# Sums for the relations' matrices made beside Wout and root instead of inside the attention, and stored by SyncE

## The reference

```python
# attention (16 heads, 256 random features), xn = layernorm(x)
q, k, v = split(xn @ Wqkv + bqkv)
out = numerator / (denominator + 1e-6)          # per head, feature map exp
x_mix = out @ Wout + bout
# relations
u = xn @ root + bias
for r in range(8):
    mask = (edge_type == r)
    sums = segment_sum(xn[src] * mask[:, None], dst)
    cnt  = segment_sum(mask, dst)
    u = u + (sums / maximum(cnt, 1)[:, None]) @ weight[r]
z = concat([u, xn]) @ w_gate + b_gate
x = x + tanh(u) * z + xn * (1 - z) + x_mix
```

## Time and profile before

| | |
|---|---|
| median of three executions | 3250.0 us |
| lowest, highest | 3239.06, 3251.52 us |
| the profiled execution's time | 3249.8 us |
| its span | 3248.0 us |
| its mean granted TensorE clock | 0.94 of full speed |

### The profile page before, as it was taken

One profiled execution on the slowest core, in us unless ns is written; L12 is line 12 of the kernel. 1 busy time (PEld: TensorE's weight loads), 2 busy tenths in 40 slices (PEclk: granted clock), 3 DMA queues, 4 the chain that ended last, 5 costly groups with the idle time before them and its releaser, 6 DMA issues.

```text
span 3248.0 us, 39307 instructions
## 1 busy us (share of the span) xinstructions
PE 2798.1 (86%) x16055; PEld 2453.6 (76%) x16055; DVE 1869.4 (58%) x2046; ACT 1321.4 (41%) x1721; POOL 582.8 (18%) x535
## 2 busy tenths in 40 slices
PE   4766798899999999999556777779899999999988
PEld 3654587877777777776556766677899999999987
DVE  5438924587877887777725555554244444444443
ACT  1315512266667676667235555541111111112221
POOL 3775400100000000000105555540100000000000
PEclk7889998999999999999768888889999999999999
DMA  4150011699999999989543333443332222113211
GB/s 133 48 139 4 1 48 46 187 320 332 327 323 330 339 325 320 332 313 327 134 169 97 108 102 101 108 116 109 111 90 72 72 72 72 52 52 136 72 60 68
DMA packets 163910, 500.77 MB, mean 154 GB/s; under 512 B 45615, under 2 KB 58287, under 8 KB 162470
## 3 DMA queue, kind: packets, MB, share of 16 engines
q1 hardware_dynamic: 98698, 389.85, 34.6%
q0 software_dynamic: 49312, 74.20, 9.1%
q10 hardware_dynamic: 15722, 34.22, 3.0%
HBM read 425.52 MB, written 72.39 MB: 153 GB/s over the span
## 4 chain that ended last, share of the span: by engine, by line
PE 66%; DVE 9%; ACT 7%; POOL 6%; DMA 5%; issue 4%; another core or an unknown queue 3%; ACTq 0%; SPq 0%; DVEq 0%; POOLq 0%
PE ps L188 65%; POOL scr_edges L926 3%; DMA er<-in_wd 3%; DVE es_l L213 2%; DVE T_l L213 1%; ACT es_h L655 1%; POOL lc L1253 1%; ACT et L2016 1%; DVE acc L209 1%; ACT lh L1213 1%; DMA wr<-in_Wq 1%; POOL scr_adj L1880 1%; DVE x L201 1%; ACT kp_h L2017 1%
## 5 line engine op out<-in xcount | busy, mean ns | idle before, releaser
L213 DVE TENSOR_TENSOR es_l<-er,es_h 128x1408 fp32r<-128x1408 f32 (+1 forms) x455 | 653.1, 1445 | 187.4 <-ACT es_h L655 183.9
L655 ACT ACTIVATE es_h<-er 128x1408 fp32r<-128x1408 f32 (+1 forms) x455 | 563.3, 1242 | 264.7 <-PE ps L188 185.3
L188 PE MATMUL ps<-T_h,ws_h 128*128 128x314 f32 x1856 | 439.5, 319 | 35.1 <-DVE ws_l L213 24.5
L655 ACT ACTIVATE ws_h<-wr 128x1024 fp32r<-128x1024 f32 (+1 forms) x181 | 190.5, 1053 | 631.8 <-PE ps L188 564.0
L188 PE MATMUL ps<-T_h,ws_l 128*128 128x314 f32 x1856 | 432.2, 315 | 0.0
L188 PE MATMUL ps<-T_l,ws_h 128*128 128x314 f32 x1856 | 431.9, 315 | 0.0
L188 PEld LDWEIGHTS ps<-T_h,ws_h 128*128 128x128 f32 x1856 | 325.4, 199 | 40.3 <-issue 28.0
L213 DVE TENSOR_TENSOR ws_l<-wr,ws_h 128x1024 fp32r<-128x1024 f32 x165 | 204.4, 1240 | 233.9 <-ACT ws_h L655 232.0
L188 PEld LDWEIGHTS ps<-T_l,ws_h 128*128 128x128 f32 x1856 | 323.9, 197 | 0.0
L188 PEld LDWEIGHTS ps<-T_h,ws_l 128*128 128x128 f32 x1856 | 322.5, 197 | 0.0
L188 PE MATMUL ps<-es_h,xe_h 128*98 128x512 f32 (+1 forms) x768 | 208.0, 379 | 9.9 <-DVE es_l L213 6.9
(11 more groups left out here) (395 smaller groups left out, 5489.8 us busy)
## 6 DMA issues: line engine op xcount, KB each, us to landing
er<-in_wg SPq DMA_DIRECT2D x128, 704.0 KB, 6.7
er<-in_wu SPq DMA_DIRECT2D x128, 704.0 KB, 5.9
er<-in_wd SPq DMA_DIRECT2D x176, 512.0 KB, 5.1
wr<-in_rel SPq DMA_DIRECT2D x64, 512.0 KB, 3.7
wr<-in_Wqkv SPq DMA_DIRECT2D x24, 512.0 KB, 7.0
steps<-scr_adj POOLq DMA_DIRECT2D x8, 1533.2 KB, 23.8
wr<-in_gate SPq DMA_DIRECT2D x16, 512.0 KB, 3.5
wr<-in_w SPq DMA_DIRECT2D x14, 512.0 KB, 3.5
```

The lines of the kernel that those rows point to most:

```text
L188: return e.matmul(out, l, r, start=start, stop=stop, skip_group_check=True)
L213: return e.tensor_tensor(lo, src, hi.bitcast(F32), ALU.subtract)
L655: q.e.activation(c.hi, c.at, ACT.Copy).then_inc(*self.s("high").up(c.key))
```

## The change

- The tallies leave the attention. They go into slots: one slot after each group of three matmuls (a block and a node tile) of `Wout`, 80 in all, and one after each of the eight steps k of a `root` output, 64 in all. Chunk c takes slot c + 8, so the last one takes slot 130 of 144, in the seventh root output.
- While `Wout` runs, a tally takes two single banks of the three that are left, and VectorE sums each half by itself (`tally_halves`). From slot 80 on it takes an aligned pair, and the sum is one instruction.
- `blocks()` goes through the 16 weight chunks (8 of Wout, 8 of root) with the tallies that fall to each. ScalarE makes the `bod` of the next block ahead. `bod` has six buffers and `blc` eight, `acc` four as before.
- The low parts of seven of these 16 chunks are made by GpSimd (`pool=`, `p_low`).
- SyncE stores the sums: `reg_load` of the row number into a register, then a plain DMA to `d_adj[ds(v, 125), :]`. The stores of a block stand in SyncE's program between the loads of weight chunks. `brows` now holds the first row of each block alone.
- x stays in its place; its copy, the reload and `scr_x` are gone. The tally's buffers lie in R3 instead. The edges' table `seb` is read after the attention's last feature (`p_tallies`).
- ScalarE issues the loads of `nat` directly after the attention (its `a_attention` no longer ends with Wout's splits).
- GpSimd's load of `steps` and the first mean wait until all stores have landed.
- bout is added as a column in the gate (`gated`, one scalar operand more) and no longer as a row on x.

```diff
@@ memory @@
-        X = self.oX
         for i in range(4):
-            at(f"bod{i}", X + i * 1280, NT, BF16)
-            at(f"blc{i}", X + 5120 + i * 256, 128, BF16)
-            at(f"acc{i}", X + 6144 + i * 2528, NT)
+            at(f"acc{i}", R3 + 20224 + i * 2528, NT)
+        for i in range(6):
+            at(f"bod{i}", R3 + 30336 + i * 1280, NT, BF16)
+        for i in range(8):
+            at(f"blc{i}", R3 + 38016 + i * 256, 128, BF16)
@@ weights @@
-                W.add(("Wout", h, i), W2(a["Wout"], 2 * i, 2 * i + 2, h), 1024, 2)
+                W.add(("Wout", h, i), W2(a["Wout"], 2 * i, 2 * i + 2, h), 1024, 2, pool=i % 2 == 0 and h + i > 0)
-            W.add(("root", o), a["root"][o], 1024, 2)
+            W.add(("root", o), a["root"][o], 1024, 2, pool=o % 2 == 0)
@@ sync, for each weight chunk @@
+            n = self.W.of[c.key] - self.W.of["Wout", 0, 0] - 4
+            if 0 <= n < 16:
+                self.s_store_tallies(q, [*blocks[n - 1][2][3:], *blocks[n][2][:3]] if n else blocks[n][2][:3])
+            elif n == 16:
+                self.s_store_tallies(q, blocks[15][2][3:])
@@ new @@
+    def blocks(self):
+        keys = [("Wout", h, i) for h in range(2) for i in range(4)] + [("root", o) for o in range(KD)]
+        n = 0
+        for b, key in enumerate(keys):
+            size = 10 if b < 8 else 8
+            yield b, key, [c for c in range(n - 8, n + size - 8) if 0 <= c < NCH]
+            n += size
+    def s_store_tallies(self, q, chunks):
+        e, m = q.e, self.m
+        for c in chunks:
+            q.wait_ge(self.s("slots"), "rows")
+            e.reg_load(self.slots[c % 4], m["brows"][0:1, c:c + 1])
+            v = e.snap(self.slots[c % 4], min_val=0, max_val=(NBK + NCH) * TP)
+            for i, _, _ in self.tally_halves(c):
+                q.wait_ge(*self.ps.done(("tally", c), i))
+            e.dma_start(self.d_adj[bass.ds(v, TP), :], m[f"acc{c % 4}"][0:TP, :]).then_inc(*self.landed(f"tally{c % 4}").up(c))
@@ t_tally @@
+        if slot < 80:
+            bs = ps.take(("tally", c), 2)
+        else:
+            b, = ps.take(("tally", c), 1, 2)
+            bs = [b, b + 1]
...
+            ins = mm(q.e, ps.one(bs[h], TP, 0, H), m[f"blc{c % 8}"][:, 0:TP], m[f"bod{c % 6}"][:, h * H:(h + 1) * H], True, True)
@@ p_attention becomes p_tallies @@
-        e.dma_start(self.d_x, self.x).then_inc(*self.landed("x_kept").up(0))
...
-                e.indirect_dma_start(self.d_adj, to, m[f"acc{c % 4}"][0:TP, :], None).then_inc(*self.landed(f"tally{c % 4}").up(c))
...
-        e.dma_start(self.x, self.d_x).then_inc(*self.landed("x_back").up(0))
@@ v_relations @@
+        for b, key, chunks in self.blocks():
...
+            for i in range(max(len(chunks), 5)):
+                if b == 4 and i < T:
+                    self.v_add_x1(q, ("Wout", 0), 0, i)
+                if i < len(chunks):
+                    self.v_tally(q, chunks[i])
+                if i == 4:
+                    self.v_low(q, key)
@@ p_relations @@
         q.wait_ge(self.s("product"), ("Wout", 1, 3))
+        for i in range(4):
+            q.wait_ge(self.landed(f"tally{i}"), NCH - 1 - (NCH - 1 - i) % 4)
@@ v_gate @@
-            tt(e, m[f"t3{o % 2}"], t1, t2, ALU.add).then_inc(*self.s("gated").up(o))
+            stt(e, m[f"t3{o % 2}"], t1, m["bcol"][:, 48 + o:49 + o], t2, ALU.add, ALU.add).then_inc(*self.s("gated").up(o))
```

More of the change, by code:

```diff
@@ L704, in t_trn, with t_nat @@
             ins = mm3(q.e, outs, (hi[:, c], lo[:, c]), self.Tk(k, name), k == 0, k == KD - 1)
-        ins.then_inc(*self.s("product").up(key))
-    def t_nat(self, q, name, h, nk, lhs, ready=None, more=()):
+            if k == KD - 1:
+                ins.then_inc(*self.s("product").up(key))
+            if slot is not None:
+                self.t_tally(q, slot + k)
+        self.ps.held = set()
+    def t_nat(self, q, name, h, nk, lhs, ready=None, more=(), slot=None):
         group = (name, *more, h)
+        if slot:
+            was = self.ps.group[(name, *more, 0)]
+            self.ps.held, self.ps.next = set(range(8)) - set(was), was[0]
         bs = self.ps.take(group, T)
+        if slot is not None:
+            self.ps.held = set(bs)
         for i in range((nk + 1) // 2):
@@ L1826, in v_tally @@
+    def v_tally(self, q, c):
         m, ps = self.m, self.ps
[L1827 to L1834, removed]
+        acc, was = m[f"acc{c % 4}"][0:TP, :], m[f"acc{(c - 1) % 4}"][0:TP, :]
+        q.wait_ge(self.s("tallied"), c)
+        if c > 3:
+            q.wait_ge(self.landed(f"tally{c % 4}"), c - 4)
+        for i, cut, src in self.tally_halves(c):
+            shape = two if len(src.shape) == 3 else (lambda z: z)
@@ L1835, in v_tally @@
             if c:
-                q.wait_ge(*ps.done(("tally", c - 1)))
-                ins = stt(q.e, two(acc), two(was), m["same"][0:TP, c:c + 1], src, ALU.mult, ALU.add)
-            else:
-                q.wait_ge(self.landed("x_kept"), 0)
-                ins = q.e.tensor_copy(two(acc), src)
-            ins.then_inc(*ps.out(("tally", c)))
+                for j, _, _ in self.tally_halves(c - 1):
+                    q.wait_ge(*ps.done(("tally", c - 1), j))
+                ins = stt(q.e, shape(acc[:, cut]), shape(was[:, cut]), m["same"][0:TP, c:c + 1], src, ALU.mult, ALU.add)
+            else:
+                q.wait_ge(self.s("attended"), 7)
+                ins = q.e.tensor_copy(acc[:, cut], src)
@@ L1843, in v_slots @@
+            ins.then_inc(*ps.out(("tally", c), i))
     def v_slots(self, q):
@@ L2298, in a_relations @@
             e.dma_start(m[b][0:TP, :].bitcast(F32), self.d[n][0:TP, :]).then_inc(*self.landed("norm_by_nodes").up(i))
[L2299 to L2302 removed]
+        blocks = list(self.blocks())
+        for b, key, _ in blocks:
+            self.a_high(q, key)
+            if not b:
+                self.a_signs(q, blocks[0][2])
+            ahead = blocks[b + 1][2] if b < 15 else []
+            self.a_signs(q, ahead[:6])
+            if b > 7:
+                self.a_root(q, b - 8)
+            self.a_signs(q, ahead[6:])
         for r in range(8):
```

203 lines of the change are left out of this document (87 added, 116 removed).

## The result

The kernel after takes 3316.53 us (median of 3 runs, 3312.0 to 3331.26), the kernel before 3250.0. The ratio is 1.0225 with a 95% interval of 1.0165 to 1.0286: the change makes the kernel slower, clear of noise, by some 2%. The forecast was 3354 with a range of 3262 to 3450. The profiled execution of after is the median one, with a span of 3314.7 us.

A forecast was written before the change was run, and what follows sets the result against it. No engine was full: attention's TensorE waited in order for tally operands; after the move, five DMA engines would pace the stores. 3249.8 - 6 (copy of x) - 140 (attention) + 250.6 (Wout-root stage) = 3354 us, range 3262 to 3450.

The forecast's parts named there:

- The sign and its cause: Whole kernel: slower (chance 0.82), since direct 125-row stores in Wout and root run on five DMA engines, 2.43 us each.
- The attention's term: Attention without its tallies: 17.5 us a round won, 140 us in all, bounds 82 and 263, practical end 190.
- no chain of ScalarE, then VectorE, then TensorE allows: Attention: upper bound of 33 us a round or 263, with every idle microsecond, pairs and clock drops gone, held unreachable.
- eight rounds of 18 tallies: Attention: 18 tallies taken out of each round; 17.5 us a round was counted as 140 us in all.
- The copy of x: Ahead of the attention: dropping the copy shortens ScalarE's wait for the norms' stores by 6 us, bounds 0 and 19.
- The stage: Start of Wout to the count-in: 375.7 us in place of 125.1, +250.6; stores 299, reload 38, weights 17, end 21.7.
- are covered by the same 2.43: Wout and root: stores' waits block loads queued behind them in SyncE, but add nothing beyond 2.43 us a store.
- the engines alone would go at some 1.1 us a tally: Wout with slots: compute engines' pace for `blc`, `bod`, pair and sum, with 0.73 us of Wout between slots.
- my 1.6 for the engines: Wout and root: 1.6 us a tally, as pair, semaphores and first half of a sum come in turn in three banks.
- The register: SyncE's register load before each store: between nothing and 1.25 us, under the 2.43 of the transfer either way.
- The rival that pays: Wout and root: stores spread over 16 engines, 1.6 us a tally, stage 227 us, kernel 3206 us; chance 0.14.
- What was to show it: Signs: attention rounds some 52 us, clock above 0.9, DMA share near 0.33, `acc` 2.4 us apart, `steps` in 16 us.

The follow-up runs named there:

- The last two experiments: Kernel before, tallies kept but nothing stored: 3197.93 us; the same with TensorE's tally matmuls also taken out: 3098.36 us.
- the first experiment: Changed kernel with each sum stored by two DMAs, of 112 and 13 rows, in place of one of 125: 3218.21 us, ratio 0.9911.
- the kernel before with cuts: Kernel before, tallies left in the attention, norms' stores, their reload and `steps` cut into 112 and 13 rows: 3212.77 us, ratio 0.9883.
- the kernel with all cuts: Changed kernel with tally stores, norms' stores, reload and `steps` cut into 112 and 13 rows, row registers loaded by eight: 3147.05 us, ratio 0.9692.

## Why the prediction was right and where it was off

**The sign and its cause were right.** The stores run on five engines: share 0.32 to 0.38, and cutting 125 into 112 and 13 raises it to 0.55, and to 0.74 from 2030 to 2040 us once the register loads are out of the way. The Trainium skill's rule ("DMA: Bandwidth & Descriptors", section "Why a DMA increments its semaphore by 16 and not by 1") agrees with both; here it held for a store addressed by a register too (0.34 at 121 GB/s).

**The attention's term was too small.** The forecast had 140 us for the tallies out of the attention, and 216.4 came. The step that was off is the count of waits: "Of the 88.4 us of waits I leave 12.5 ... 76 over the attention, 9.5 a round", and with it the claim that taking every idle microsecond of a round is what "no chain of ScalarE, then VectorE, then TensorE allows". Pairs and clock drops together were sized about rightly: TensorE's busy time fell by 13.9 us (50.84 to 36.94) where I had 4.8 + 7.9 = 12.7. But its idle time fell from 20.2 to 1.1, not by 9.5. I had read the waits that TensorE spent ahead of tally matmuls and left those ahead of other operands as the attention's own. Without tallies they were gone too, so they were the tallies' as well: a `bod` stands ahead of an `et` in ScalarE, a sum ahead of a split in VectorE. The last two experiments price the groups, not each such pair: of 32 us a round some 8 are GpSimd's stores, 15 TensorE's, 9 the other engines' time. Nothing of it came back, where I had let 4.5 us a round come back, since without tallies TensorE is busy for 36.9 of 38 us.

The sum also has eight rounds of 18 tallies, and that is wrong: 123 tallies fill 6.8. From copy to copy six rounds of before take 69.8 us each, the first one, with fewer tallies, takes 63.3, and from the last copy to Wout it is 31.4, where it is 29.8 with no tallies at all. 6.8 times the measured 32 is 218. So per tallied round the gap is larger than the totals show, 32 against 17.5, and the eight rounds hid a part of it.

**The copy of x:** 6 taken. From the first issue of a norms' store to the first attend's copy 8.6 us came (73.9 to 65.3), within the bounds of 0 and 19; the other 2.3 of the 10.9 lie ahead of it. Only 2.8 is the shorter wait that I argued from. Most lies in ScalarE's issues, which I had not looked at: the second and third no longer take over 2 us. The stretch is 73.7 to 74.0 in the three kernels of before without tallies, stores or tally matmuls, which all keep the copy, and 65.2 to 65.3 in the five variants of after with uncut norms' stores, which have none. The copy was not taken out alone, so that it is the cause is likely and not shown.

**The stage was dearer.** +293.7 in place of +250.6. The end was exact (16.20 and 5.41 for 16.1 and 5.4). The start, 1976.89 to 2021, took 44 us with the first two stores in it, where I had 38 for the reload and 5 for two stores. The other 121 stores landed from 2021 to 2373: 352 us, 2.91 each, and the forecast had (299 + 17) / 123 = 2.57 with the weights. So 41 us are to be told there.

About half is the rate of the store itself. Where no weight load is beside them, sums come 2.59 us apart (nine sums start from 2034.58 to 2055.29) at 121 GB/s. I had 2.43 at 129, the rate of `steps`, which has the same shape but is a read. That is 0.17 for each of 121, 21 us.

The engines also ran dry, but for less than it seems: in windows of one microsecond their share falls short of five engines by some 8 us in all, and 5 of these are one hole. The DMA rate over 2022 to 2140 us in 40 slices, and SyncE around the hole:

```profile
GB/s 137 120 125 116 119 122 119 123 119 121 120 167 149 114 121 121 121 121 120 122 147 218 122 120 119 122 118 123 119 112 94 0 85 151 110 115 118 118 122 120
...
2083.30 25.68 SPq L1934 DMA_DIRECT2D scr_adj<-acc  x10
2117.34 0.38 SPq L641 DMA_DIRECT2D wr<-in_root  x1
2118.50 22.55 SPq L1934 DMA_DIRECT2D scr_adj<-acc  x10
```

VectorE had ended two sums at 2112.3 and 2116.2, but their stores stand in SyncE's program behind a weight load, and SyncE stood 8.3 us in front of that load (from 2109.0 to 2117.3) until VectorE had made a low part (2116.09, 1.22 us). Sums came 3.85 us apart ahead of the hole, since VectorE adds Wout's first half to x between them, so the queue was nearly empty by then. GpSimd's split of 2.34 us, for which TensorE does wait, left no hole: beside the one from 2079.74 to 2082.08 the share stayed at 0.32 and the rate at 118 GB/s or more, as stores were still queued.

The last 12 us I did not take apart. A sum near a weight load comes 1.2 to 3.0 us late, where the forecast had 1.2 a load, so a part of it is probably there. My line that the waits of the loads "are covered by the same 2.43" holds but for the hole.

The forecast's "the engines alone would go at some 1.1 us a tally" was seen with cut stores and eight registers, 1.13 us for stretches, but from 2027 us to the last sum at 2236.6 the average was 1.8 a tally, so my 1.6 for the engines was too low by a little as well.

**The two errors have opposite signs**, 76 + 5 against 43, which is why 3316.5 lies only 37.5 below the forecast and inside its own range of 3290 to 3400. The direction follows from the mechanism; that the number came so near is partly luck. **The register** was priced rightly for this kernel (under the transfer), and my bound of 1.25 us held for the median (0.80) but not for the longest load (2.2); it only shows once the transfer is spread. **The rival that pays** (3206) did not happen. Cut stores gave 3218, but that its price comes near is luck: it had 146 won and a stage of 227 us, and the cut kernel won 226 ahead of Wout and had a stage of 316, with SyncE and not the engines as the pace.

**What was to show it.** Rounds of some 52 us: 37.8, outside what I gave. Clock above 0.9: 1.00. DMA share near 0.33: 0.34 to 0.38 from 2022 us on, at 121 to 137 GB/s in place of 130 to 140. `steps` in 16 us: 16.2. `acc` 2.4 us apart: 2.6. TensorE idle for over half: no, 42% of 2022 to 2140, at a clock of 0.64, so that its busy time is itself stretched.

## What to carry to other kernels

Before moving transfers into a stage, ask how many DMA engines their shape uses: the share over a window with only such transfers tells it (0.32 for 125 rows), and a cut into a part that spreads and a short rest can be worth more than the move. To price work taken out of a busy stage, don't sum the waits of the engine that is on the path; the removed work's small instructions in the other engines' programs delay it as well, and a run without the work gives the true price (207 us in the time here, 218 over the attention; the forecast was 140). Take a transfer's rate from one in the same direction as well as of the same shape: the stores went at 121 GB/s where a load of that shape had gone at 129. And where one engine's program issues loads and stores, look what a wait ahead of a load (8.3 us here) holds up behind it.

## What the hardware showed that I had not expected

- Two DMAs of 112 and 13 rows went every 1.13 us in bursts of up to five tallies, where one of 125 rows goes every 2.6: 2.3 times the rate for the same bytes. From 2027 us to the last sum it was one tally in 1.8 us.
- A register load from SBUF on SyncE takes 0.45 to 2.2 us (median 0.80 in after, 0.81 in the first experiment), one that fills eight registers 1.1 in the median (0.73 to 1.7). A DMA issue of this kind takes 0.29 to 0.35 as a rule, but beside the norms' reload two of them took 17.3 and 11.8 us in after.
- The issue of a DMA on ScalarE took from 0.26 to 6.55 us; the first norms' store of a kernel was always issued quickly (0.26 to 0.32), most of the later ones were not. Cutting transfers made this worse: 16.0 us for the six issues in the kernel before with cuts, 9.3 for four in before, 3.1 in after, 12.5 for six in the kernel with all cuts.
- TensorE kept the full clock (2.4 GHz) through whole rounds of 38 us, in which its pauses were 0.44 and 0.58 us. In the tallied Wout, idle for 42% of the time, it had 0.64 of it on average: the five matmuls of one slot took 1.15 us at the higher level and 2.03 at the lower. There it cost nothing, since both lie inside the 2.6 us of a store.
